# A windowed top-k attention with relative positions: the loop's body becomes a whole batch, outputs of eight head pairs accumulate in one PSUM bank, tables are read in place, and one matmul makes both heads' relative products

## The reference, cut to what matters

```python
scores = einsum('bhid,bhjd->bhij', q, k) * SCALE          # 16 heads of 64, n = 512
dist = clip(coords[:, None] - coords[None, :], -64, 64) + 64
scores = scores + einsum('bhid,ijd->bhij', q, rel_k_emb[dist])
threshold = top_k(scores, 32)[0][..., -1:]
attn = softmax(where(scores < threshold, -inf, scores))
for i in range(3):                                         # v_curr starts as v
    a_v = einsum('bhij,bhjd->bhid', attn, v_curr)
    if i == 0:
        a_v = a_v + einsum('bhij,ijd->bhid', attn, rel_v_emb[dist])
    v_curr = a_v
    res = res + alphas[i] * v_curr
out = res (heads side by side) @ Wout.T + bout
```

## Time and profile before

| | us |
|---|---|
| median of 3 runs | 3138.28 (3134.51 to 3139.64) |
| profiled execution, its own time | 3144.04 |
| its span | 3142.3 |

### The profile page before, as it was taken

The page is one execution under the profiler, slowest core; times in us unless marked ns, Lnnn a source line. Parts: engine busy times, 40 slices in busy tenths (PEclk is TensorE's granted clock), DMA queues, the critical chain, the costliest instruction groups (busy, mean ns, idle before and its releaser), DMA issues. The chain is left out here.

```text
span 3142.3 us, 66621 instructions
## 1 busy us (share of the span) xinstructions
PE 2607.6 (83%) x15200; PEld 1498.6 (48%) x15200; DVE 2719.1 (87%) x6639; ACT 2027.7 (65%) x6207; POOL 2163.7 (69%) x2732
## 2 busy tenths in 40 slices
PE   4788888888788888888888888888888685988857
PEld 2444444444444444444444444444444444777743
DVE  5999999999999999999999999999998374765646
ACT  2677777877777777777777777777787152222214
POOL 1788888888888888888888888888888142221105
PEclk7899999999999999999999999999999696776659
DMA  4444444444444444444444444444443000000001
GB/s 119 118 132 134 129 127 125 129 132 125 131 126 129 127 127 127 128 126 130 131 129 126 130 125 134 125 125 131 127 131 100 4 29 14 8 6 1 0 8 48
DMA packets 401017, 318.44 MB, mean 101 GB/s; under 512 B 33246, under 2 KB 388648, under 8 KB 400808
## 3 DMA queue, kind: packets, MB, share of 16 engines
q1 hardware_dynamic: 398660, 314.18, 34.7%
q10 hardware_dynamic: 2148, 2.33, 0.3%
HBM read 139.48 MB, written 136.58 MB: 88 GB/s over the span
## 5 line engine op out<-in xcount | busy, mean ns | idle before, releaser
L870 DVE MAX8 top<-work 128x8 f32<-128x512 f32 x1536 | 980.7, 681 | 0.0
L880 DVE MATCH_REPLACE8 work<-top,work 128x512 f32<-128x512 f32 x1024 | 685.5, 678 | 0.0
L949 POOL TENSOR_TENSOR scores<-scores,cut 128x512 f32<-128x512 f32 x512 | 643.7, 1279 | 0.0
L562 PE MATMUL bank<-probs_t,u 128*64 128x512 f32 x2048 | 467.7, 598 | 1.4 <-ACT u L760 1.4
L794 ACT ACTIVATE probs_of_tile<-scores,minus_max_and_least 128x512 f32<-128x512 f32 x512 | 373.9, 748 | 89.7 <-POOL scores L949 89.2
L959 POOL TENSOR_SCALAR probs_of_tile<-probs_of_tile,inverse 128x512 f32<-128x512 f32 x512 | 349.0, 692 | 84.1 <-DVE inverse L845 61.4
L867 DVE MAX8 top<-scores 128x8 f32<-128x512 f32 x512 | 325.9, 679 | 82.8 <-issue 63.5
L940 POOL TENSOR_SCALAR cut<-scores,minus_max_and_least 128x512 f32<-128x512 f32 x512 | 354.2, 692 | 62.7 <-issue 39.5
L880 DVE MATCH_REPLACE8 work<-top,scores 128x512 f32<-128x512 f32 x512 | 342.7, 678 | 0.0
L771 ACT ACTIVATE probs_t<-bank 128x512 f32<-128x512 f32 x512 | 283.6, 609 | 66.7 <-PE bank L646 66.5
L945 POOL TENSOR_SCALAR cut<-cut 128x512 f32<-128x512 f32 x512 | 305.8, 613 | 21.5
(11 more groups left out here) (251 smaller groups left out, 5062.7 us busy)
## 6 DMA issues: line engine op xcount, KB each, us to landing
probs_scratch<-probs_of_tile SPq DMA_DIRECT2D x256, 256.0 KB, 2.5
band<-probs_scratch SPq DMA_DIRECT2D x256, 256.0 KB, 3.2
rel_scratch<-rel SPq DMA_DIRECT2D x256, 254.0 KB, 3.1
relj<-rel_scratch SPq DMA_DIRECT2D x256, 128.0 KB, 2.3
relj<-rel_scratch SPq DMA_DIRECT2D x512, 64.0 KB, 2.5
xt<-stream_normed_t SPq DMA_DIRECT2D x64, 256.0 KB, 2.4
pair_j<-table_j SPq DMA_DIRECT2D x64, 193.5 KB, 2.2
pair_o<-table_o SPq DMA_DIRECT2D x64, 66.0 KB, 1.9
```

The source lines that it names most:

```text
L562: last = nc.tensor.matmul(U[HEADS[h], :], lhs, pt[mpar][:, h, jt, :], start=(jt == 0), stop=(jt == NT - 1 and step > 0))
L870: nc.vector.max(top[q][:, h, 8 * r:8 * r + 8], work[:, h, :]).then_inc(s.next_tops, 1)
L880: nc.vector.match_replace(out=work[:, h, :], in_to_replace=top[q][:, h, 8 * r:8 * r + 8], in_values=sc[Tc][:, h, :] if r == 0 else work[:, ...
L949: nc.gpsimd.tensor_tensor(sc[Tc][:, h, :], sc[Tc][:, h, :], cut[:, h, :], ALU.add).then_inc(s.masked, 1)
```

## The change

It does five things.

1. The loop's body is a whole batch, eight iterations: after one iteration of straight code, `batch(0)` is straight code as well, then come 6 passes of the loop, `batch(7)` and three more iterations as straight code. The pair's number is now known when the code is written.
2. The tables are therefore read in place: `pair_j`, `pair_o` and their DMAs are gone, and only `xt` is still copied.
3. The output products of a batch's eight pairs accumulate in bank 3 (`OUT`), and DVE adds them to the stream once per batch instead of once per iteration.
4. The relative products of both heads come from one matmul over all 128 rows: `rel_keys` is now 128 x 508 with zeros where a head meets the other's columns, set up once.
5. ACT copies these products with one instruction of 508 columns instead of two of 254.

```diff
-    def __init__(self, g, par, T):
-        self.g, self.par, self.i, self.T = g, par, g * 2 + par, T
+    def __init__(self, g, c, T):
+        self.g, self.c, self.i, self.T = g, c, g * PAIRS + c, T
 
     def half(self, d):
 
-        return self.g + (self.par + d) // 2
+        return self.g * (PAIRS // 2) + (self.c + d) // 2
+
+    def pair(self, d):
+
+        return (self.c + d) % PAIRS
...
 def run_iterations(eng, body):
 
 
-    first, last = 4, ITS - 2
-    for i in range(-1, first):
-        for T in range(NT):
-            body(Slots(i // 2, i % 2, T), i % 2)
-    with eng.Fori(first // 2, last // 2) as g:
-        for par in range(2):
+    for T in range(NT):
+        body(Slots(-1, PAIRS - 1, T), 1)
+
+    def batch(g, count=PAIRS):
+        for c in range(count):
             for T in range(NT):
-                body(Slots(g, par, T), par)
-    for i in range(last, ITS + 3):
-        for T in range(NT):
-            body(Slots(i // 2, i % 2, T), i % 2)
+                body(Slots(g, c, T), c % 2)
+
+    batch(0)
+    with eng.Fori(1, B - 1) as g:
+        batch(g)
+    batch(B - 1)
...
-    SC, RL, PT, U, MISC = ps[0:2], ps[2:4], ps[4:6], ps[6], ps[7]
+    SC, RL, OUT, PT, U, MISC = ps[0:2], ps[2], ps[3], ps[4:6], ps[6], ps[7]
     HEADS = [slice(h * DH, (h + 1) * DH) for h in range(2)]
+
+    def batch_of(z):
+
+        return z.g + (z.c - 3) // PAIRS
 
     def mixing(z, par):
 
         T, old, av = z.T, z.iteration(-3), z.iteration(-2)
         if T == 3 and av is not None:
-            return av, 1, par
+            return av, 1, par, z.pair(-2)
         if T < 2 and old is not None:
-            return old, T + 2, 1 - par
+            return old, T + 2, 1 - par, z.pair(-3)
         return None
...
             def body(z, par):
                 T, q = z.T, z.T % 2
                 if T == 2 and (it := z.iteration(1)) is not None:
-                    at_pair, at_batch = known(sp, (it % PAIRS) * J_COLS, (it // PAIRS) * N)
-                    c0 = known(sp, it - 1)[0]
+                    at_batch, c0 = known(sp, (z.g + (z.c + 1) // PAIRS) * N, it - 1)
                     if not early(c0):
                         sp.wait_ge(s.v_kept, c0)
-                    sp.dma_start(pj[1 - par][:, :], t.TJf[:, bass.ds(at_pair, J_COLS)]).then_inc(s.pj_in[1 - par], 16)
-                    sp.dma_start(xt[1 - par][:, :], t.XNT[:, bass.ds(at_batch, N)]).then_inc(s.pj_in[1 - par], 16)
-                if T == 3 and (it := z.iteration(-1)) is not None:
-                    at_out, = known(sp, (it % PAIRS) * O_COLS)
-                    c0 = known(sp, it - 1)[0]
-                    if not early(c0):
-                        sp.wait_ge(s.out_made, c0)
-                    sp.dma_start(po[1 - par][:, :], t.TOf[:, bass.ds(at_out, O_COLS)]).then_inc(s.po_in[1 - par], 16)
+                    sp.dma_start(xt[1 - par][:, :], t.XNT[:, bass.ds(at_batch, N)]).then_inc(s.xt_in[1 - par], 16)
...
-                    for h in range(2):
-                        last = nc.tensor.matmul(RL[h][:, 0:2 * NEAR], qt[par][HEADS[h], Ta * P:(Ta + 1) * P],
-                                                t.relk[HEADS[h], :], start=True, stop=True)
-                    last.then_inc(s.rel_made, 1)
+                    nc.tensor.matmul(RL[:, 0:4 * NEAR], qt[par][:, Ta * P:(Ta + 1) * P],
+                                     t.relk[:, :, :].rearrange("p h c -> p (h c)"),
...
                     if T == 0 and cur is not None:
                         pe.wait_ge(s.q_kept, cur + 1)
-                    if T == 3 and old is not None:
-                        pe.wait_ge(s.out_added, old + 1)
-                    elif T == 3 and prev is not None:
...
                 if T == 2 and old is not None:
                     pe.wait_ge(s.res_chain, old * 5 + 5)
-                    pe.wait_ge(s.po_in[1 - par], 16 * (z.half(-3) + 1))
-                    if prev is not None:
-                        pe.wait_ge(s.v_kept, prev + 1)
+                    pair = z.pair(-3)
+                    if pair == 0 and not early(batches := batch_of(z)):
+                        pe.wait_ge(s.out_added, batches)
                     for jt in range(NT):
-                        last = nc.tensor.matmul(MISC[:, jt * P:(jt + 1) * P], res[:, jt * P:(jt + 1) * P],
-                                                po[1 - par][:, O_W:O_W + P], start=True, stop=True)
+                        last = nc.tensor.matmul(OUT[:, jt * P:(jt + 1) * P], res[:, jt * P:(jt + 1) * P],
+                                                t.TO[:, pair, O_W:O_W + P], start=(pair == 0 and jt == 0),
+                                                stop=(pair == PAIRS - 1 and jt == NT - 1))
...
-                    pe.wait_ge(s.pj_in[par], 32 * (z.half(0) + 1))
+                    pe.wait_ge(s.xt_in[par], 16 * (z.half(0) + 1))
                     pe.wait_ge(s.q_kept, cur + 1)
                     if m:
                         pe.wait_ge(s.u_kept, m[0] * 2 + 2)
-                    nc.tensor.matmul(MISC[:, :], pj[par][:, J_WK:J_WK + P], xt[par][:, :],
+                    nc.tensor.matmul(MISC[:, :], t.TJ[:, z.pair(0), J_WK:J_WK + P], xt[par][:, :],
...
-                    for h in range(2):
-                        last = nc.scalar.activation(rel[sp2][:, h, :], RL[h][:, 0:2 * NEAR], ACT.Copy)
-                    last.then_inc(s.rel_kept, 1)
+                    nc.scalar.activation(rel[sp2][:, :, :].rearrange("p h c -> p (h c)"), RL[:, 0:4 * NEAR],
...
-                    if old is not None and T == 2:
+                    if old is not None and T == 2 and z.pair(-3) == PAIRS - 1:
                         dve.wait_ge(s.out_made, old + 1)
-                        if not early(old):
-                            dve.wait_ge(s.out_added, old)
-                        Xb = k.X[:, bass.ds((old // PAIRS) * N, N)]
-                        nc.vector.tensor_tensor(Xb, MISC[:, :], Xb, ALU.add).then_inc(s.out_added, 1)
+                        Xb = k.X[:, bass.ds((z.g - 1) * N, N)]
+                        nc.vector.tensor_tensor(Xb, OUT[:, :], Xb, ALU.add).then_inc(s.out_added, 1)
```

More of the change, by code:

```diff
@@ L288, in _ @@
                 nc.vector.memset(t.prob[T][:, :, HALF + N:PADDED], 0.0)
+            for s in range(2):
+                nc.vector.memset(t.relk[(1 - s) * DH:(2 - s) * DH, s, :], 0.0)
             dve.wait_ge(w_in, 16 * LOADS)
@@ L308, in _ @@
                                     relv0_col[:, 0:1], None, ALU.add)
-            nc.vector.tensor_scalar(t.relk[:, NEAR:2 * NEAR], ps[5][:, 1:P], relk0[:, 0:1], None, ALU.subtract)
+            for s in range(2):
+                half = slice(s * DH, (s + 1) * DH)
+                nc.vector.tensor_scalar(t.relk[half, s, NEAR:2 * NEAR], ps[5][half, 1:P], relk0[half, 0:1], None,
+                                        ALU.subtract)
             nc.vector.tensor_scalar(column(t.TJ[:, :, J_BKR:J_BKR + 1]), ps[4][:, PAIRS:2 * PAIRS],
@@ L312, in _ @@
             dve.wait_ge(chain, 4)
-            nc.vector.tensor_scalar(t.relk[:, 0:NEAR], ps[5][:, 1:P], rel_last[:, 0:1], None, ALU.subtract)
+            for s in range(2):
+                half = slice(s * DH, (s + 1) * DH)
+                nc.vector.tensor_scalar(t.relk[half, s, 0:NEAR], ps[5][half, 1:P], rel_last[half, 0:1], None,
+                                        ALU.subtract)
             nc.vector.tensor_scalar(column(t.TJ[:, :, J_BKL:J_BKL + 1]), ps[4][:, PAIRS:2 * PAIRS],
@@ L424, in attention @@
     s.bias_added = sem("att_bias_added")
-    s.pj_in = [sem(f"att_pj_in{q}") for q in range(2)]
-    s.po_in = [sem(f"att_po_in{q}") for q in range(2)]
+    s.xt_in = [sem(f"att_xt_in{q}") for q in range(2)]
     s.rel_stored = [sem(f"att_rel_stored{q}") for q in range(2)]
@@ L614, in body @@
                         pe.wait_ge(s.q_kept, cur + 1)
-                    if T == 3 and old is not None:
-                        pe.wait_ge(s.out_added, old + 1)
-                    elif T == 3 and prev is not None:
+                    if T == 3 and prev is not None:
                         pe.wait_ge(s.v_kept, prev + 1)
@@ L662, in body @@
                         last = nc.tensor.matmul(MISC[:, jt * P:(jt + 1) * P], xt[1 - par][:, jt * P:(jt + 1) * P],
-                                                pj[1 - par][:, J_WV:J_WV + P], start=True, stop=True)
+                                                t.TJ[:, z.pair(-1), J_WV:J_WV + P], start=True, stop=True)
                     last.then_inc(s.v_made, 1)
                 if T == 3 and nxt is not None:
-                    pe.wait_ge(s.pj_in[1 - par], 32 * (z.half(1) + 1))
+                    pe.wait_ge(s.xt_in[1 - par], 16 * (z.half(1) + 1))
                     if m:
@@ L670, in body @@
                         pe.wait_ge(s.v_kept, prev + 1)
-                    nc.tensor.matmul(MISC[:, :], pj[1 - par][:, J_WQ:J_WQ + P], xt[1 - par][:, :],
+                    nc.tensor.matmul(MISC[:, :], t.TJ[:, z.pair(1), J_WQ:J_WQ + P], xt[1 - par][:, :],
```

(21 more changed lines are left out.)

10 lines of the change are left out of this document (5 added, 5 removed).

## The result

The changed kernel takes 3248.55 us (median of 4 runs, 3240.88 to 3273.25) against 3138.96 us for the kernel before (4 runs beside it, 3134.51 to 3143.19). The ratio is 1.036, with an interval of 1.030 to 1.042: 110 us slower. 3112 us was forecast, between 3044 and 3140. The profiled execution took 3242.43 us with a span of 3240.7 us, 98 us more than before.

A forecast was written before the change was run, and what follows sets the result against it. DVE was taken as the bound at 37.00 us an iteration, with a PE, ACT and SP cycle taking over at 36.45: 31 us gained over 56 iterations, less 5 for jumps, 26 us, so 3112 us, range 3044 to 3140.

The forecast's parts named there:

- The bound before: DVE sets the pace at 37.00 us an iteration, its stalls at the loop's head being code that arrives late.
- the second cycle: Through PE, ACT and SP, without DVE or POOL: 35.05 us an iteration, rising to 36.0 and then setting the pace.
- the five links: From one T = 2 band sum to the next: 8.61, 8.94, 8.79, 4.86 and 3.85 us.
- The additions and the jumps: DVE's 64 stream additions become 8, at 0.6 us each; five loop jumps left cost 1 us each, 5 in all.
- the term for the low clock: PE at half clock about 5% of an iteration, hitting products with V: 0 to 0.9 us, taken as 0.45.
- rival C: No change: merged product and PE's clock at the upper side of their bounds, 36.9 us an iteration, 3138 us; chance 0.11.
- The middle of the bounds: For PE's low clock, 0.45 us an iteration was taken between 0 and 0.9, giving 36.45 us.
- rival B: Low clock in every iteration, at products with V after PE's band wait: 1.72 us each, 3183 us; chance 0.11.
- The merged product: One 508-column matmul lengthens PE's part of slots T = 3, 0 and 1: 0.45 us extra per slot, 0.9 plus 0.1 together.
- The link through SP: In T = 1, SP stores `rel`, only then loads `band`, for which ACT's next band sum waits: 3.85 us.
- Rival A: DVE stays the bound, the merged product costing PE about what the pair did or hiding in a wait: 3045 us; chance 0.18.
- Rival D: Longer loop body makes code late inside a pass too, on an engine of the cycle: 3179 us; chance 0.04.

The follow-up runs named there:

- the swap: Changed kernel with SP starting the load of `band` ahead of the store of `rel`: 3051.37 us, ratio 0.9740; second series 3052.05 us.

## Why the prediction was wrong

*The bound before, and the second cycle behind it.* Right, and the best part of it. The cycle has the five links named, it became the bound, DVE lost its lead and waits for scores, and opening it at SP's order is worth 197 us.

*The additions and the jumps.* Right as far as they went: 0.6 us was forecast for an addition, and 27.7 / 56 = 0.5 measured once DVE was the bound again. The 5 us for the jumps were too much while the cycle is the bound: the five iterations with a jump take 40.4 us on average, but the ones behind them 37.5, and together that is two mean iterations, so the stall is given back.

*"So it runs at 1.2 instead of 2.4 GHz for about 5% of 37 us."* This is the step that failed: the term for the low clock, 0.45 us in an iteration in the forecast, measured 2.03 us, 1.72 of it in the products with V. Its size was wrong in two ways. The first is the reading of the row. At half clock a stretch takes only half off the mean. A mean of 0.95 says that PE is at 1.2 GHz for 10% of the time, 3.7 us of an iteration, and can lose up to 1.85 us of work, not 0.9. The upper bound was half of what the row says. With this put right and the middle kept, the sum would be 36.0 + 0.9 = 36.9 us, which is rival C's 3138 us and still no loss.

*The middle of the bounds.* The second is the place. The prediction took the middle, although it had named the place and seen the wait move there ("what is late next at that place is the turned band"). A mean over the whole loop doesn't tell on which instructions the low clock falls. Before, the wait for `res` stood ahead of short transposes with time to spare; now a wait as long stands ahead of V. The first link is 2.03 us over its least, 1.72 of it in V. This is rival B's mechanism at rival B's price, and B had a chance of 0.11. That the price agrees to the last digit is luck: B took it from two iterations, and single ones lose from nothing to 2.8 us. Against B stood one wait of 2.89 us without a loss. That was one iteration; over iterations 6 to 56 the loss is the rule, 48 to 3.

*The merged product.* Right in its mechanism, too small in its size: 1.0 us forecast, and by the medians 0.6 (T = 3), 0.67 (T = 0) and 0.3 us (T = 1), 1.6 in all. Each slot pays 0.6 and not 0.45. The 0.21 us that ACT was to hide in T = 1 it did hide: from the start of `relj` to its copy of the scores it is 0.94 us before and 0.70 after (medians). The 0.14 in T = 0 it hardly did: 0.85 and 0.81. The Trainium skill, "TensorEngine Tiling (Array Packing)", Tiling Modes, says that changing the mode drains the array. The runs agree with a small price for it, 0.09 us on either side.

*The link through SP.* 4.09 us on average for the 3.85 of one iteration: 0.24 more.

The sum with the terms that were measured: 36.45 forecast + 1.6 (clock, 2.03 for 0.45) + 0.6 (product) + 0.24 (SP) = 38.9, against 38.98 us.

The experiments agree with this. Rival A asked for a product that hides: it hides, but only once the cycle is open. Rival D is refuted: the merged product is as slow in the short body, and with the swap the same long body runs half of its iterations in 34.6 to 34.9 us. What isn't settled: why an idle time of 3 us leaves the clock alone in 3 of these 51 iterations (8.68 us in the first link) and not in the others.

## What to carry to other kernels

Before work is taken from the engine that is full, follow the next cycle through every queue, SP's order of DMAs among them: a load behind a store that it doesn't need cost nothing that could be told while DVE was the bound, and 197 us after. A mean granted clock of 1 - x means 2x of the time at half clock, and its price depends on what follows the wait, so when an edit moves a wait, take the price at the new place and over many iterations. Where the cycle can't be opened, idle products in the wait can give most of the clock's price back, here 102 of 110 us.

## What the runs showed of the hardware

- All five engines stall at a jump back over the long body. In the changed kernel, between the branch and the next instruction of the loop's head, it is 2.8 to 3.1 us on DVE, 2.6 to 3.1 on ACT, 3.3 to 4.0 on POOL, 3.6 to 4.4 on PE, 2.7 to 2.8 on SP. With two iterations in the body only DVE did (2.8 to 4.0 us), and the others took 0.24 to 0.33 us. PE hides most of it behind work it has already queued; POOL doesn't. Behind one jump:

```profile
960.93 0.81 PE L584 MATMUL bank<-keys_left,qt 64*128 64x320 f32 x4 [0.85 <-issue]
```

```profile
963.52 0.69 POOL L914 TENSOR_SCALAR tmp<-mixed,table_o 128x512 f32<-128x512 f32 x1 [2.64 <-issue]
```

  Where DVE is the bound such a jump costs some 3 us: 8.5 / 3 = 2.8 by the two profiled executions, 11.5 / 3 = 3.8 by medians that are not clear of noise.
- The clock fell with PE's one wait of 3.1 to 4.7 us in 48 of 51 iterations, and it cost 1.72 us of each on average in one group of products. Nearly as many microseconds of useless products in the wait (3.60) gave back 102 us.
